# Other places and PSUM banks for side stages in a two-layer attention and feed-forward kernel on one NeuronCore

## The reference

```python
x = x + L0_xattn(layernorm(x), ctx, mask)      # 32 query heads, 8 key heads of 128, RoPE
x = x + L0_ffn(layernorm(x))                   # silu(h@Wg) * (h@Wu) @ Wd, inner size 1376
x = x + L1_xattn(layernorm(x), ctx, mask)      # rmsnorm(q), rmsnorm(k), softmax, no RoPE
x = x + L1_ffn(layernorm(x))                   # top 8 of 128 slots, gate from an uncertainty

def dequant(qw, qz, sc, g):                    # W = sc[g] * (nibble(qw) - nibble(qz) - 1)
    return sc[g] * (nibbles(qw) - (nibbles(qz)[g] + 1.0))
```

## Time and profile before

| | |
|---|---|
| median of 3 runs | 2674.35 us (2670.53 to 2675.8) |
| profiled execution: time | 2667.68 us |
| profiled execution: span | 2665.9 us |
| PE busy in the span | 2515.9 us (94%) |
| DVE, ACT, POOL busy | 1804.5, 1179.7, 1061.2 us |
| PE idle before an instruction, windows 1240 to 2600 us, longest kinds | DVE L1866 6.4, DVE L1525 6.1, DVE L1904 4.6 us |
| mean granted TensorE clock | 0.978 of full speed |

### The profile page before, as it was taken

The page is one execution under the profiler, slowest core; times in us unless marked ns, Lnnn a source line. Parts: engine busy times, 40 slices in busy tenths (PEclk is TensorE's granted clock), DMA queues, the critical chain, the costliest instruction groups (busy, mean ns, idle before and its releaser), DMA issues. The chain is left out here.

```text
span 2665.9 us, 45902 instructions
## 1 busy us (share of the span) xinstructions
PE 2515.9 (94%) x18339; PEld 1389.5 (52%) x18339; DVE 1804.5 (68%) x3271; ACT 1179.7 (44%) x2281; POOL 1061.2 (40%) x844
## 2 busy tenths in 40 slices
PE   7799999999999998799999889999999999999987
PEld 3355555555555554334444455655665565555543
DVE  7687787778787778434443556677777767765665
ACT  4555555555455444322221364444444444443333
POOL 3454445554455544122222243333333433333332
PEclk9899999999999999899999999999999999999999
DMA  6000010000010001100110100010010001000001
GB/s 192 17 25 17 33 41 9 33 9 33 10 40 17 2 4 37 33 24 1 32 49 11 40 17 1 1 33 25 25 33 9 33 9 33 25 15 1 1 1 64
DMA packets 57254, 68.73 MB, mean 26 GB/s; under 512 B 9858, under 2 KB 32966, under 8 KB 57040
## 3 DMA queue, kind: packets, MB, share of 16 engines
q1 hardware_dynamic: 57044, 65.79, 7.8%
HBM read 61.59 MB, written 4.19 MB: 25 GB/s over the span
## 5 line engine op out<-in xcount | busy, mean ns | idle before, releaser
L729 PE MATMUL PB<-WB,AR 128*128 128x512 f16 x3072 | 700.0, 382 | 24.5 <-issue 9.7
L685 PE MATMUL PB<-XTB,WB 128*128 128x512 f16 x3072 | 691.7, 383 | 3.4 <-DVE XTB L1598 3.4
L685 PEld LDWEIGHTS PB<-XTB,WB 128*128 128x128 f16 x3072 | 300.7, 99 | 352.9 <-issue 18.6
L729 PEld LDWEIGHTS PB<-WB,AR 128*128 128x128 f16 x3072 | 295.2, 98 | 360.4 <-issue 32.5
L1762 DVE SCALAR_TENSOR_TENSOR X<-PB,SML,X 128x512 f32<-128x512 f32 x256 | 191.5, 749 | 212.9 <-PE PB L729 206.5
L2248 POOL TENSOR_TENSOR AR<-AR,SML 128x512 f32<-128x512 f32 x128 | 144.7, 1152 | 331.8 <-DVE SML L1732 331.8
L1246 ACT ACTIVATE AR<-PB 128x512 f16<-128x512 f32 x256 | 132.3, 600 | 246.9 <-PE PB L768 246.9
L1666 DVE TENSOR_TENSOR AR<-PB,AR 128x512 f16<-128x512 f32 x128 | 87.6, 688 | 160.6 <-ACT AR L1216 160.1
L844 PE MATMUL PB<-XTB,AR 128*128 128x512 f16 (+1 forms) x864 | 195.6, 384 | 0.0
L2268 POOL TENSOR_TENSOR SML<-SML 128x16 f32<-128x16 f32 x32 | 98.1, 3065 | 239.6 <-DVE SML L1674 239.6
L2242 POOL TENSOR_TENSOR AR<-AR 128x512 f32<-128x512 f32 x128 | 184.4, 1441 | 22.3 <-DVE AR L1632 13.6
(11 more groups left out here) (222 smaller groups left out, 4014.0 us busy)
## 6 DMA issues: line engine op xcount, KB each, us to landing
STG<-in_wo SPq DMA_DIRECT2D x14, 1024.0 KB
STG<-in_wq SPq DMA_DIRECT2D x13, 1024.0 KB
STG<-in_qw_gu SPq DMA_DIRECT2D x40, 128.0 KB
STG<-in_ctxT SPq DMA_DIRECT2D x4, 1024.0 KB
X<-in_x SPq DMA_DIRECT2D x4, 1024.0 KB, 10.8
out_x<-X SPq DMA_DIRECT2D x16, 256.0 KB, 2.4
STG<-in_wk SPq DMA_DIRECT2D x14, 256.0 KB
STG<-in_wv SPq DMA_DIRECT2D x14, 256.0 KB
```

Of the source, the lines that this page charges most:

```text
L685: m = pe.do.matmul(b[:, :], wq[x][:, k, h * 128:(h + 1) * 128], XT[y][c][:, k, :], start=n == 0, stop=n == 11)
L729: m = pe.do.matmul(b[:, :], AT[x][:, h, t * 128:(t + 1) * 128], wo[y][:, h, :], start=n == 0, stop=n == 11)
```

## The change

Nothing is added or taken away; stages move and banks are exchanged.

- Slices 1 to 3: `amax` one slot later, `peak` behind `gate_up` of chunk 3 and `scale` behind the two `down` tiles after it, `low` in the two slots that follow, the second of them in the next slice. For w(1, 1, 0) in slice 5 `peak` and `scale` are each a slot later.
- `down` of slice 5 puts tiles 2 and 3 into banks 2 and 3.
- The keys and values of unit 1 in layer 1 are computed before `scores(0)`, around `turn_k(0)`.
- Unit 0 of layer 1: the norm stages of chunk 1 are later, `peak` of w(1, 1, 2) goes to slot 8, `scale` and `low` to unit 1.
- Tail, chunks 0 and 1: `t_turn`, the second `t_norm` and `t_q` a slot later; third and fourth turned tile in banks 1 and 6; `t_lg` in bank 6, `t_turn_w(0)` in bank 6.

```diff
-        plan_ln(1, 0, 2, 1, False)
-        plan(1, 0, 0, "peak", w(1, 1, 2), 6)
-        plan(1, 0, 1, "scale", w(1, 1, 2), 7)
+        for slot, *stage in ((1, "ln_norm", 0), (4, "ln_turn", 0), (5, "ln_low", 0), (5, "ln_norm", 1), (7, "ln_turn", 1),
+                             (8, "ln_low", 1)):
+            plan(1, 0, slot, stage[0], 2, 1, stage[1])
+        plan(1, 0, 8, "peak", w(1, 1, 2), 3)
+        plan(1, 1, 0, "scale", w(1, 1, 2), 7)
         for half in range(2):
-            plan(1, 0, 2 + half, "low", w(1, 1, 2), half)
+            plan(1, 1, 1 + half, "low", w(1, 1, 2), half)
...
-                (u - 1, 9, ("t_stats", c)), (u, 1, ("t_norm", c, 0)), (u, 2, ("t_turn", c, 0)), (u, 3, ("t_norm", c, 1)),
-                (u, 5, ("t_turn", c, 1)), (u, 7, ("t_q", c)), (u + 1, 1, ("t_up", c)), (u + 1, 1, ("t_rq", c)),
+                (u - 1, 9, ("t_stats", c)), (u, 1, ("t_norm", c, 0)), (u, 3, ("t_turn", c, 0)), (u, 4, ("t_norm", c, 1)),
+                (u, 6, ("t_turn", c, 1)), (u, 8, ("t_q", c)), (u + 1, 1, ("t_up", c)), (u + 1, 1, ("t_rq", c)),
...
-        TB_TURN = {0: (2, 3, 0, 1), 1: (2, 3, 0, 1), 2: (6, 7, 6, 7), 3: (6, 7, 1, 3)}
+        TB_TURN = {0: (2, 3, 1, 6), 1: (2, 3, 1, 6), 2: (6, 7, 6, 7), 3: (6, 7, 1, 3)}
-        TB_R, TB_A, TB_LG, TB_W = (2, 2, 7, 7), (3, 3, 1, 1), (2, 2, 4, 2), (2, 2, 4, 4)
+        TB_R, TB_A, TB_LG, TB_W = (2, 2, 7, 7), (3, 3, 1, 1), (6, 6, 4, 2), (6, 2, 4, 4)
...
-            plan_prep_f(w(1, 0, s - 1), (s, 2, 2), (s, 2, 3), (s, 3, 0), (s, 3, 2), (s, 3, 3))
+            plan_prep_f(w(1, 0, s - 1), (s, 2, 3), (s, 3, 1), (s, 3, 2), (s, 3, 3), (s + 1, 0, 0))
-        plan_prep_f(w(1, 1, 0), (5, 0, 3), (5, 1, 0), (5, 1, 1), (5, 1, 3), (5, 2, 0))
+        plan_prep_f(w(1, 1, 0), (5, 0, 3), (5, 1, 1), (5, 1, 2), (5, 1, 3), (5, 2, 0))
...
+        def down_bank(s, t):
+
+            return 6 + t % 2 if s < 5 or t < 2 else t
...
-                    b = bank(6 + t % 2, (x_add, ("f", s, c, t)))
+                    b = bank(down_bank(s, t), (x_add, ("f", s, c, t)))
...
-                else:
+                elif u > 1:
                     keys_values(u, 0)
                     keys_values(u, 1)
...
+            keys_values(1, 0)
             turn_k(0)
+            keys_values(1, 1)
             norm_q(0)
```

More of the change, by code:

```diff
@@ L1865, in down @@
                     dve.wait_ge(*added[c, t])
-                    dve.do.scalar_tensor_tensor(xs, PB[6 + t % 2][:, :], CY[:, :], xs, ALU.mult, ALU.add
+                    dve.do.scalar_tensor_tensor(xs, PB[down_bank(s, t)][:, :], CY[:, :], xs, ALU.mult, ALU.add
                                                 ).then_inc(x_add.of(("f", s, c, t)), 1)
```

## The result

| | before | changed | ratio |
|---|---|---|---|
| median | 2674.35 us (3 runs) | 2652.27 us (4 runs, 2650.85 to 2654.05) | 0.9919, 95% interval 0.9905 to 0.9933 |
| profiled execution: time | 2667.68 us | 2653.32 us | |
| its span | 2665.9 us | 2651.5 us | |
| mean granted clock | 0.978 | 0.977 | |

The account below looks back on a forecast made before the run. PE, busy 94% of the span, was taken as the bound. The terms summed to -18.1 us, from 2667.68 to 2649.6 for the profiled execution; adding its 6.7 distance below the median gave 2656.3 us, range 2642 to 2668.

Parts of the forecast that it names:

- Slices 1 and 2: Moved weight stages in the feed-forward: waits for peak and scale go, new bank 6 waits come; +2.5 and -2.7 us.
- Slice 3: Moved weight stages, with no load behind low that PE wants soon: waits and slow matmuls go, -3.9 us (to -2.4).
- w(1, 1, 0): Weight in slice 5: its 3.04 us wait goes, the turning behind waits 1.1 us longer for LNB; -2.1 us left.
- what is late next: Working method at each place: shift PE earlier by what is removed, move the producers, see who is last then.
- Four banks: down in slice 5: the DVE wait only moves to the first keys (0), the last down stops waiting; -1.4 us.
- Unit 0: Second attention, keys ahead and stages moved: about 5 us wait at turn_k, scores of unit 1 earlier; -3.3 us.
- Unit 27: Tail: LNB and bank 0 waits and slow matmuls go (-5.6), t_q before weigh costs 0.8; -4.8 us.
- Unit 29: Tail: the bank 2 wait goes, query head 2 waits 2.7 us for bank 6 and slows; net -0.8 us.
- the covers hold: Rival for the whole kernel: the returning waits are short or absent, about -38 us, 2636 us; chance 0.22.
- It doesn't do what it says: Rival for the whole kernel: every wait returns at the next instruction and slows the clock; -4, 2670 us; chance 0.10.
- SP's queue decides: Rival in slices 1 to 3: late low parts delay loads; 12 us more lateness loses 24 us; chance 0.04.
- Cycling through banks: Rival in the last slice: four down banks beside two for gate_up slow the clock, 42 us lost, 2698; chance 0.02.

## Why the prediction was right

The median came out 4 us below the forecast, inside the range. The parts of these 4 us: -0.3 from the stretches behind the first edit (-18.4 against -18.1), +4.05 from the stretch ahead of it, -6.7 since the prediction added the distance of before's profiled execution from its median, and -1.1 since the changed kernel's profiled execution lies above its median. That the terms add up to within 0.3 us is in part luck: four of them are off by 1.5 to 2 us, two each way, and nearly cancel, and what the profiled execution shows of the clock behind a wait changes from one execution to the next.

- **Slices 1 and 2.** The chain POOL, SP, DMA, DVE, bank 6 was as worked out: 2.79 for 3.2 and 2.21 for 2.0 us of wait. The term's slow clock came behind the second wait and not the first, so slice 1 gave +0.5 for +2.5 and slice 2 -0.9 for -2.7; together -0.4 for -0.2. The loads moved in SP's list show the mechanism. From the `down` of slice 1, chunk 2, to slice 4 it took 170.6 us before and 166.0 in this profile; in eight other profiled executions with the same code there 163.7 to 166.3, so the gain of 4.6 is at the low end.
- **Slice 3** gave -4.1 for -3.9.
- **w(1, 1, 0)** failed by its size: -0.6 for -2.1. The 3.04 went and the turning's wait grew by 1.45 (from 1.15 to 2.60, where 1.1 was worked out), but behind it 12 `down` took 4.99 instead of 2.9 us (2.75 to 5.05 in the other twelve profiles, behind waits of 2.3 to 2.6). The step "what is late next" priced the wait without the clock that it might cost.
- **Four banks** gave -1.4 as predicted: the wait for DVE passed to the first keys (3.56), which stayed slow. But the size is luck of this execution. From the last `gate_up` to the queries it takes 22.6 us with two banks (in the kernel before, and again with the banks put back), and with four, in eight profiled executions, 20.8 to 22.3, since the keys take 6.7 to 8.3 us: 0.3 to 1.8 us are gained, 1.0 on average. That the statistics cause the wait was shown; they were worth more than the banks.
- **Unit 0** gave -3.35 for -3.3, with the 5.03 at the turning of k where 5 was worked out. But the prediction did not say which part pays: all of it comes from the moved stages, and the keys ahead bring nothing beside them (and cost some 3 us without them).
- **Unit 27** -4.9 for -4.8, `t_lg` -1.96 for -1.6.
- **Unit 29** was mis-sized: -2.65 for -0.8. The wait at bank 6 was 2.64 (2.7 predicted), but no slow clock followed it. In three of nine profiles one did.

The rivals: *the covers hold* is out, since each of its five waits appeared. *It doesn't do what it says* and *SP's queue decides* are out by the table; the queue cost 5 to 7 us, not 24. *Cycling through banks*: the 96-row `down` in banks 6, 7, 2, 3 runs 12 matmuls in 2.75 and 2.91 us, at full clock, wherever no wait stands just ahead. By the rule of the Trainium skill, "TensorE: Matmul & The Clock Gate", section "A second HAM failure mode: psum-queue depth-cycling", the sum would have been +24; the trace does not bear it out here.

## What to carry to other kernels

Where a hand-written order is shifted, follow the producers past every in-order queue: the gain at PE was paid back wherever a load, a low part or a copy stood behind the moved stage, and SP's list was the cheapest thing to mend. Then undo each part alone: one of five parts here brought nothing, and its better form was half of it. And read an experiment of some microseconds by the stretch that it changes as well as by its median, and that stretch in more than one profiled execution.

## What was not expected

The same wait, before the same turning in unit 27, cost the clock in one kernel and not in another. Columns: window, its length, then busy us (instructions) of PE, PEld, DVE, ACT and POOL, PE's granted clock, DMA share, GB/s. The kernel before, and then the changed kernel with the tail back:

```profile
2415.00:2421.00 6.00, 3.42 (x16) 1.37 (x14) 6.00 (x16) 5.06 (x13) 2.35 (x3) 1.00 0.00 0
2421.00:2429.00 8.00, 7.88 (x33) 3.81 (x34) 1.90 (x4) 2.67 (x5) 7.37 (x7) 0.79 0.00 0
```

```profile
2408.00:2414.00 6.00, 3.66 (x17) 1.47 (x15) 6.00 (x15) 4.86 (x13) 2.10 (x3) 1.00 0.00 0
2414.00:2422.00 8.00, 7.63 (x44) 4.46 (x45) 3.58 (x6) 4.18 (x9) 7.92 (x7) 1.00 0.00 1
```

The waits are 2.70 and 2.71 us and the work ahead is the same; in the first the clock then stood at 0.79 on average, between its levels of 2.4 and 1.2 GHz, for 24 query matmuls in 7.03 us, in the second at 1.00 for 5.34. In the same way two waits of 1.3 and 1.1 us in slice 1 slowed `gate_up` in one kernel (7.04) and not in another (5.35), and waits of 2.79 and 2.64 us had full clock behind them, while those of 2.21 and 3.56 had not. The clearest case is the query head of unit 29 behind bank 6, since its wait is 2.63 or 2.64 us in all nine profiled executions that have it. In six its 12 matmuls take 2.76 us, in three 4.15 to 4.28, as with the loads later in SP's list:

```profile
2485.61 4.15 PE L691 MATMUL PB<-XTB,WB 128*128 128x512 f16 x12 [2.63 <-ACT XTB L1378]
```

Likewise `down` in slice 3 was slow behind waits of 2.07, 2.18, 2.21, 2.54 and 2.56 us and at full clock behind 1.64, 1.74, 1.83 and 2.14, and `down` in slice 2 was at full clock behind 2.66 to 2.79 us in all nine. So the length of a wait of 1 to 3 us does not tell here whether the clock falls behind it. Charging 1.7 us for some of the waits was right in the sum, by luck, and wrong in four single places. What decides it was not tried.
